# Spline stage with six result buffers, x added by a transfer, and one mask block in eight made on ScalarE

## The chip, the cores and the metric

The kernel runs on one core of one Trainium2 chip. The metric is the device time of one execution in microseconds (us). A core has TensorE (PE in the profile), VectorE (DVE), ScalarE (ACT), GpSimd (POOL) and SyncE (SP), each with its own instruction stream in program order. They share SBUF, wait for each other through semaphores, and data moves by DMA, which SP, ACT or POOL issue.

## The reference

The input x is 32 images of 64 channels and 56 x 56 pixels. Everything is float32.

```
out = relu(batchnorm(conv3x3(x, sign(w1))))          # statistics over all images
z   = relu(batchnorm(conv3x3(out, sign(w2))) + x)
u   = (clip(z * a + b, -1.5, 1.5) + 1) * 0.5 * 31     # a, b per channel
i, t = floor(u), u - floor(u)
y_nl = sum over 4 neighbours of table[channel, i + k] * cubic_k(t)
out = id_gain * z + y_nl + bias                       # per channel
```

The table of a channel is `alpha_table` (32 x 8) times that channel's row of `mix`. So the last layer is a cubic spline with 32 knots and a different table in each channel, applied to 6.4 million values.

## The kernel before

**Two convolutions, then the spline.** Images are taken in 16 pairs, 128 partitions = 2 images x 64 channels. Each convolution sums its taps in PSUM, and its result goes to a scratch array in DRAM (`y1_scratch`, `y2_scratch`). Both end in a short batch norm on VectorE. The second one's scale and bias are needed before any spline value can be made. At 427 us of 1252.8 the spline stage begins, and nearly all of the change is in it.

**Chunks.** The spline works on 32 chunks, each half of an image pair: 128 partitions x 1568 pixels. A chunk's value is a polynomial of third degree in the distance `offset` from one of 17 centres, with an extra cubic term for distances over 1 (`far`). The five coefficients (tables) of each pixel depend on which centre is nearest. They are found without a gather: 16 masks say whether the pixel lies past step s, and TensorE adds up mask times step height. The masks stand in four tiles ("quads") of 128 partitions x 4 blocks x 1568 pixels: a block holds 32 of the 128 (image, channel) rows, and the four groups of 32 partitions hold four different steps. For this the cell number of each pixel (`cell`) is first copied by 16 small DMAs into `cell4` (the spread).

**One table.** `product` (line 1177) multiplies a mask tile by diagonal weights in two parts (high and low half of the step). Tables NEAR and FAR use all four quads (128 matmuls each per chunk), SQ, LIN and VAL only the two edge quads (64 each). Two PSUM areas `tab` alternate, so table number n may begin only when VectorE has read table n-2 (`table_used`, line 1200). VectorE then computes with the sum, reading PSUM directly.

**VectorE's order for chunk c** (`body`, line 1149): VAL of chunk c-1 (1090), `finish` of c-1 (1121), `total` of c+2 (1016: y times scale plus x), `near_cube` (1067), `fixed` and `linear` of c+2 (1022, 1028), `far_cube` (1075), `far_part` (1083), both middle masks of c+1 (1045), SQ (1090), `near_part` (1098), `slope` (1105), `add_slope` (1113), `offsets` of c+2 (1037).

**ScalarE's order** (line 993): `far_distance` of c (961), `position` of c+2 (930), `far_square` (968), `cells` of c+2 (938), `distance_square` (975), `distance` of c+1 (954), two edge masks of c+1 as signs (982). A sign is -1 or 1 where a mask is 0 or 1. So the edge weights are half the step, and half of all such steps is added to the constant `first`.

**GpSimd** issues one accumulating DMA per chunk, which adds `far` to `lin` (919). `far_distance` of the next chunk overwrites `far` and waits for it to land. **SP** issues for each chunk the store of the chunk before, the loads of y (into `zbuf`) and x (into one of four `lin` buffers), then the 16 spread DMAs.

Of the kernel before, what the change touches and what calls it, by code (L numbers as in the profile page):

```python
# [49 lines left out]
QUAD_ORDER = MIDDLE_QUADS + EDGE_QUADS  # L50
QUADS_OF = (QUAD_ORDER, QUAD_ORDER, EDGE_QUADS, EDGE_QUADS, EDGE_QUADS)
GROUP = 32
BUFS = 4
# [32 lines left out]
def convolutions(nc, sem, keep, wts, par_dram, mix_t, alpha_t, x, y1, y2):  # L86
# [3 lines left out]
    with ExitStack() as ctx:  # L90
# [44 lines left out]
        stored = [sem(f"y_stored{b}") for b in range(2)]  # L135
# [36 lines left out]
        x_first = x[0]  # L172
# [52 lines left out]
        def _(sp):  # L225
# [60 lines left out]
            for b in range(2):  # L286
                sp.wait_ge(stored[b], 32 * half_rounds)

        @block.gpsimd
        def _(pool):  # L290
# [20 lines left out]
            for q in range(QUADS):  # L311
                for g in range(4):
                    above = SHIFT + 2 * (step_at(q, g) + 1)
                    link(pool.memset(thr[g * GROUP:(g + 1) * GROUP, q:q + 1],
                                     0.5 - above if q in EDGE_QUADS else above))
                    link(pool.memset(keep["above"][g * GROUP:(g + 1) * GROUP, q:q + 1], above))
# [25 lines left out]
            pool.wait_ge(steps_ready, 1)  # L342
            for t in range(TABLES):
# [13 lines left out]
        def _(act):  # L357
# [78 lines left out]
            act.activation(tmp[:, 5:6], row_scale[:, 0:1], ACT.Identity)  # L436
# [4 lines left out]
        def _(dve):  # L441
# [130 lines left out]
            def steps():  # L572
# [9 lines left out]
                link(dve.tensor_tensor(keep["first"][:, :], keep["plain"][:, :], halves[:, :], ALU.add), chain)  # L582
                for half in range(2):
# [193 lines left out]
def spline(nc, sem, keep, y2, x, out):  # L777

    with ExitStack() as ctx:
# [5 lines left out]
        cell4 = [sb(f"cell4{b}", [P, 4, CHUNK], BF16) for b in range(2)]  # L785
        edge_mask = [[sb(f"edge_mask{s}{q}", [P, 4, CHUNK], BF16) for q in range(len(EDGE_QUADS))] for s in range(2)]
        middle_mask = [sb(f"middle_mask{q}", [P, 4, CHUNK], BF16) for q in range(len(MIDDLE_QUADS))]
# [4 lines left out]
        dist_sq = sb("dist_sq", [P, CHUNK])  # L792
# [5 lines left out]
        stored = [sem(f"out_stored{b}") for b in range(BUFS)]  # L798
        far_added = sem("far_part_added")
        sum_ready = sem("sum_ready")  # L800
# [8 lines left out]
        dist_sq_ready = sem("dist_sq_ready")  # L809
# [16 lines left out]
        def summed(i, b, t):  # L826

            return tab[(b + t) % 2][:, :, 0:SUB]

        def mask_of(b, q):  # L830

            return edge_mask[b % 2][EDGE_QUADS.index(q)] if q in EDGE_QUADS else middle_mask[MIDDLE_QUADS.index(q)]

        def rounds(eng, body):

            def four(i, n):
                for b in range(BUFS):
                    body(i, b, n)

            last = CHUNKS // BUFS - 1  # L840
            four(0, 0)
            with eng.Fori(1, last) as i:
                four(i, None)
            four(last, last)

        def middle_masks(c):

            return (c + 1) * len(MIDDLE_QUADS) + len(EDGE_QUADS) if not isinstance(c, int) or c >= 0 else 0

        def edge_masks(c):  # L850

            return c * len(EDGE_QUADS) if not isinstance(c, int) or c >= 0 else 0

        def exists(n, b):
            return n is None or 0 <= BUFS * n + b < CHUNKS

        @block.sync
        def _(sp):
            def part(t, i, b):
                return in_front(sp, t[2 * i + b // 2][:, (b % 2) * CHUNK:(b % 2 + 1) * CHUNK])  # L860

            def load(i, b):

                ysrc = part(y2, i, b)
                xsrc = part(x, i, b)
                before, free = in_front(sp, BUFS * i + b - 1), in_front(sp, 16 * (i + b // BUFS))
                wait_past(sp, offset_ready, before)
                wait_past(sp, cell_ready, before)
                sp.dma_start(place[b % 2][:, :], ysrc).then_inc(y_loaded[b % 2], 16)
                wait_past(sp, stored[b % BUFS], free)  # L870
                sp.dma_start(lin[b % BUFS][:, :], xsrc).then_inc(x_loaded[b % BUFS], 16)

            def spread(i, b):

                c = BUFS * i + b
                made, used = in_front(sp, c + 1), in_front(sp, middle_masks(c - 2))
                used_edges = in_front(sp, edge_masks(c - 2))
                sp.wait_ge(cell_ready, made)
                wait_past(sp, mask_ready, used)
                wait_past(sp, sign_mask_ready, used_edges)  # L880
                first_two = isinstance(c, int) and c < 2
                for g in range(2 if first_two else 4):
                    for j in range(4):
                        sp.dma_start(cell4[b % 2][g * GROUP:(g + 1) * GROUP, j, :],
                                     cell[b % 2][j * GROUP:(j + 1) * GROUP, :]).then_inc(copied[b % 2], 16)

            def store(i, b):
                dst = part(out, i, b)
                made = in_front(sp, BUFS * i + b + 1)
                sp.wait_ge(whole, made)  # L890
                sp.dma_start(dst, lin[b % BUFS][:, :]).then_inc(stored[b % BUFS], 16)

            spread(0, 0)
            load(0, 2)
            spread(0, 1)

            def body(i, b, n):
                if exists(n, b - 1):
                    store(i, b - 1)
                if exists(n, b + 3):  # L900
                    load(i, b + 3)
                if exists(n, b + 2):
                    spread(i, b + 2)

            rounds(sp, body)
            dst, b = part(out, CHUNKS // BUFS - 1, BUFS - 1), BUFS - 1
            for half in range(2):
                own = slice(half * 2 * SUB, (half + 1) * 2 * SUB)
                sp.wait_ge(whole, CHUNKS + 2 * half + 1)
                sp.dma_start(dst[:, own], lin[b][:, own]).then_inc(stored[b], 16)  # L910
            for b in range(BUFS):
                sp.wait_ge(stored[b], 16 * (CHUNKS // BUFS + (b == BUFS - 1)))

        @block.gpsimd
        def _(pool):
            def add_far(c):

                pool.wait_ge(far_part_ready, 2 * c + 2)
                pool.dma_start(lin[c % BUFS][:, :], far[:, :], accum_op=ALU.add).then_inc(far_added, 16)  # L919

            for c in range(CHUNKS):
                add_far(c)
# [351 lines left out]
```

## Time and profile before

| | us |
|---|---|
| median of three runs | 1256.31 (1255.05 to 1257.22) |
| the profiled execution's own time | 1254.66 |
| its span in the trace | 1252.8 |
| VectorE busy | 1062.8 (85%) |
| TensorE matmuls busy | 1058.6 (85%) |
| ScalarE busy | 868.8 (69%) |
| GpSimd busy | 113.4 (9%) |
| TensorE's mean granted clock | 0.93 of full |

The page divides the span into 40 slices of 31.3 us. VectorE is at 5 to 8 tenths in the first third, which is the convolutions, and at 9 or more in nearly every slice after it. The granted clock of TensorE falls to 0.8 or 0.9 in the same slices. "Idle before, releaser" in a row is how long the engine stood still just before those instructions, and who ended that. Start times are us from the start of the span, and where instructions of one engine follow each other without idle time, the distance of two starts is a better price than the duration, as neighbours overlap slightly.

### The profile page before, as it was taken

The numbers are of one execution on the slowest core, as the hardware profiler recorded it, in microseconds if no ns is written. First come the engines' busy times: TensorE is split into PE (matmuls) and PEld (weight loads), VectorE is DVE, ScalarE is ACT, GpSimd is POOL, SyncE is SP. The second block draws the span as 40 slices with busy tenths as digits, with TensorE's granted clock in tenths as the row PEclk, the third lists the DMA queues.
The fourth block names the chain that finished last, engine by engine and source line by source line (L and its number), as shares of the span: only waits on it lengthen the run. The fifth ranks groups of instructions, "written<-read, shape, count | busy, mean of one in ns | idle before, by whom it ended". The sixth has DMA issues, their size and how long they took to land. (4 is left out here: it accounts for less than half of the span.)

```text
span 1252.8 us, 51454 instructions
## 1 busy us (share of the span) xinstructions
PE 1058.6 (85%) x23562; PEld 710.2 (57%) x23562; DVE 1062.8 (85%) x951; ACT 868.8 (69%) x424; POOL 113.4 (9%) x189
## 2 busy tenths in 40 slices
PE   6999996999999368887888788878887888788876
PEld 4688885788888234554545455444544545455444
DVE  5765656766666689999999999999999999999987
ACT  4454544777787267688868877887788778877881
POOL 6000000282000000000000000000000000000000
PEclk9999998999999778998989889898998989889898
DMA  7666766576777386677767766777677667776552
GB/s 227 259 257 256 276 255 225 217 277 252 271 264 300 136 235 181 183 216 194 185 189 213 196 181 193 208 192 184 189 214 192 184 197 206 194 182 197 157 114 78
DMA packets 58215, 260.85 MB, mean 208 GB/s; under 512 B 16336, under 2 KB 16336, under 8 KB 50000
## 3 DMA queue, kind: packets, MB, share of 16 engines
q1 hardware_dynamic: 52528, 230.88, 56.3%
q0 software_dynamic: 4608, 25.69, 11.0%
q8 instruction: 139, 2.28, 0.8%
q10 hardware_dynamic: 928, 1.90, 0.6%
q14 instruction: 12, 0.10, 0.0%
HBM read 104.29 MB, written 77.07 MB: 145 GB/s over the span
## 5 line engine op out<-in xcount | busy, mean ns | idle before, releaser
L1181 PE MATMUL tab<-edge_mask,diag 128*32 128x392 bf16 x10240 | 501.8, 358 | 132.6 <-DVE poly L1090 130.8
L1181 PEld LDWEIGHTS tab<-edge_mask,diag 128*32 128x32 f16 x10240 | 281.7, 104 | 339.0 <-DVE poly L1090 143.4
L982 ACT ACTIVATE edge_mask<-cell,thr 128x6272 bf16<-128x6272 bf16 x62 | 338.5, 5508 | 0.0
L711 PE MATMUL acc<-split,w 64*64 64x392 f16 x4608 | 195.9, 329 | 12.0 <-DVE w L463 10.8
L711 PE MATMUL acc<-band_split,w 64*64 64x392 f16 x4608 | 197.9, 330 | 9.4 <-ACT band_split L368 7.2
L410 ACT ACTIVATE yout<-acc 128x1568 f32<-128x1568 f32 x64 | 94.2, 1473 | 160.6 <-PE acc L711 139.4
L1181 PE MATMUL tab<-middle_mask,diag 128*32 128x392 bf16 x4096 | 183.4, 332 | 25.0 <-DVE middle_mask L1052 25.0
L711 PEld LDWEIGHTS acc<-band_split,w 64*64 64x64 f16 x4608 | 164.1, 107 | 42.9 <-issue 14.1
L711 PEld LDWEIGHTS acc<-split,w 64*64 64x64 f16 x4608 | 155.3, 107 | 51.9 <-issue 12.6
L520 DVE BATCH_NORM_STATS2 stats<-yout 128x392 f32 (+1 forms) x240 | 118.0, 555 | 60.2 <-ACT yout L410 59.4
L930 ACT ACTIVATE zbuf<-lin,cst 128x1568 f32<-128x1568 f32 x32 | 54.3, 1697 | 163.8 <-DVE lin L1016 157.9
L1181 PEld LDWEIGHTS tab<-middle_mask,diag 128*32 128x32 f16 x4096 | 107.7, 99 | 92.2 <-DVE middle_mask L1052 25.1
L919 POOL DMA_DIRECT2D lin<-far x32 | 50.0, 1564 | 897.5 <-DVE far L1083 897.5
L1090 DVE SCALAR_TENSOR_TENSOR poly<-tab,first,poly 128x1568 f32<-128x1568 f32 x61 | 112.6, 1845 | 0.1
L1045 DVE TENSOR_SCALAR middle_mask<-cell,thr 128x6272 bf16<-128x6272 bf16 x62 | 111.9, 1847 | 0.0
L486 DVE SCALAR_TENSOR_TENSOR band_split<-band_split,xin 128x1568 f16<-128x1568 f16 x30 | 52.5, 1793 | 35.0 <-ACT band_split L389 35.0
L1075 DVE SCALAR_TENSOR_TENSOR far<-tab,first,far 128x1568 f32<-128x1568 f32 x31 | 57.3, 1847 | 8.8 <-PE tab L1181 8.6
L497 DVE SCALAR_TENSOR_TENSOR split<-split,xin 128x3136 f16<-128x3136 f16 (+4 forms) x19 | 55.1, 2913 | 10.7 <-ACT split L400 10.5
L1083 DVE SCALAR_TENSOR_TENSOR far<-far,cst,far_sq 128x1568 f32<-128x1568 f32 x32 | 59.3, 1852 | 2.9
L1016 DVE SCALAR_TENSOR_TENSOR lin<-zbuf,cst,lin 128x1568 f32<-128x1568 f32 x32 | 59.0, 1846 | 3.1 <-PEq L90 3.1
L1121 DVE SCALAR_TENSOR_TENSOR lin<-poly,cst,lin 128x1568 f32<-128x1568 f32 x31 | 57.4, 1852 | 3.3
L1113 DVE SCALAR_TENSOR_TENSOR poly<-far_sq,poly 128x1568 f32<-128x1568 f32 x32 | 57.4, 1793 | 3.1
(126 smaller groups left out, 816.9 us busy)
## 6 DMA issues: line engine op xcount, KB each, us to landing
y_scratch<-yout SPq DMA_DIRECT2D x32, 1568.0 KB, 6.2
cell<-cell SPq DMA_DIRECT2D x496, 98.0 KB, 3.3
xin<-y_scratch SPq DMA_DIRECT2D x16, 1568.0 KB, 9.0
zbuf<-y_scratch SPq DMA_DIRECT2D x32, 784.0 KB, 5.9
lin<-in_x SPq DMA_DIRECT2D x32, 784.0 KB, 6.1
lin<-far POOLq DMA_DIRECT2D x32, 784.0 KB, 8.8
out<-lin SPq DMA_DIRECT2D x31, 784.0 KB, 4.1
xin<-in_x SPq DMA_DIRECT2D x15, 1568.0 KB, 9.3
```

The source lines that it names most:

```text
L410: act.activation(yout[b][:, :].rearrange("p (r k x) -> p k r x", r=2, k=TILES)[:, 2 * part:2 * part + 2], acc[:, 4 * part:4 * part + 4, 0: ...
L520: dve.bn_stats(stats[:, bass.ds(COUNTS * (g - base) + t, 1), :], yout[b][:, own]).then_inc(counted, 1)
L711: mm = pe.matmul(acc[h * C:(h + 1) * C, 2 * k + r, 0:TILE], weights[part][own, tap * C:(tap + 1) * C], image[own, first:first + ROWS, dx:d ...
L982: act.activation(mask_of(b, q)[:, :, :], cell4[b % 2][:, :, :], ACT.Sign, bias=thr[:, q:q + 1]).then_inc(sign_mask_ready, 1)
L1016: dve.scalar_tensor_tensor(out=lin[b % BUFS][:, :], in0=place[b % 2][:, :], scalar=cc(BN2_S), in1=lin[b % BUFS][:, :], op0=ALU.mult, op1=A ...
L1045: dve.tensor_scalar(mask_of(b, q)[:, :, :], cell4[b % 2][:, :, :], thr[:, q:q + 1], None, ALU.is_ge).then_inc(mask_ready, 1)
L1075: dve.scalar_tensor_tensor(out=quarters(far), in0=summed(i, b, T_FAR), scalar=base(i, b, T_FAR), in1=quarters(far), op0=ALU.add, op1=ALU.m ...
L1083: dve.scalar_tensor_tensor(out=far[:, :], in0=far[:, :], scalar=cc(AMP), in1=far_sq[:, :], op0=ALU.mult, op1=ALU.mult).then_inc(far_part_r ...
L1090: dve.scalar_tensor_tensor(out=quarters(poly[b % 2]), in0=summed(i, b, t), scalar=base(i, b, t), in1=quarters(poly[b % 2]), op0=ALU.add, o ...
L1113: dve.scalar_tensor_tensor(out=poly[b % 2][:, :], in0=far_sq[:, :], scalar=1 / POINT, in1=poly[b % 2][:, :], op0=ALU.mult, op1=ALU.add).th ...
L1121: dve.scalar_tensor_tensor(out=lin[b % BUFS][:, :], in0=poly[b % 2][:, :], scalar=cc(AMP), in1=lin[b % BUFS][:, :], op0=ALU.mult, op1=ALU. ...
L1181: mm = pe.matmul(tab[(b + t) % 2][j * GROUP:(j + 1) * GROUP, sub, 0:SUB], keep["diag"][part][:, j % 2, t, q, :], mask_of(b, q)[:, j, sub * ...
```

## The change

1. **Six result buffers.** `lin` has 6 buffers (`LIN`) instead of 4. For chunks 0 to 3 (`AHEAD`) y and x are loaded during the last convolution round, and VectorE still makes `total`. For every later chunk SP loads y straight into `lin`, ScalarE scales it in place (`scale`, new line 929), and GpSimd issues a second accumulating DMA that adds x from DRAM (`add_x`, new line 912). `position` waits for that instead of for `total`.
2. **One block of eight of the middle masks.** Block 3 of quad 3 is made on ScalarE as a sign (`shared`, new line 988). VectorE's mask of quad 3 shrinks from 6272 to 4704 elements per partition. TensorE uses the tile `shared_diag`, with half the step, for this block, and `first` gets the other half.
3. **Polynomial in another form.** `dist_sq` and ScalarE's `distance_square` are gone. VectorE adds SQ, multiplies by `offset`, adds LIN, multiplies by `offset`, adds VAL: as many instructions as before.
4. **Order.** On VectorE `finish` of c-1 comes after `linear`, and `fixed` before `near_cube`. On ScalarE the two edge masks are parted by `shared` and `distance`. On SP the store of c-1 comes after the spread of c+2 instead of before it. SP no longer waits, at the end of the convolutions, for their last stores to land. It waits for them in the spline stage behind two spreads.
5. **The rest.** The loops of the spline stage are written out. ScalarE's first activation is a square root instead of an identity. GpSimd prepares `shared_thr` and `shared_diag`, and VectorE does two small operations more in `steps`. The eight spread DMAs of chunk 1 that ScalarE issued are SP's.

```diff
@@ sync, last round of the second convolution
-                    sp.wait_ge(stored[0], 16 * (half_rounds + 1))
-                    for half in range(2):
-                        px = slice(half * CHUNK, (half + 1) * CHUNK)
-                        sp.dma_start(keep["zbuf"][half][:, :], y2[0][:, px]).then_inc(keep["y_loaded"][half], 16)
-                        sp.dma_start(keep["lin"][half][:, :], x_first[:, px]).then_inc(keep["x_loaded"][half], 16)
+                    for c in range(AHEAD):
+                        px = slice(c % 2 * CHUNK, (c % 2 + 1) * CHUNK)
+                        sp.wait_ge(stored[c // 2], 16 * (half_rounds + 1))
+                        y_to, x_to = keep["opening"](c)
+                        sp.dma_start(y_to[:, :], y2[c // 2][:, px]).then_inc(keep["y_loaded"][c], 16)
+                        sp.dma_start(x_to[:, :], x[c // 2][:, px]).then_inc(keep["x_loaded"][c], 16)
...
-            for b in range(2):
-                sp.wait_ge(stored[b], 32 * half_rounds)
@@ scalar, start
-            act.activation(tmp[:, 5:6], row_scale[:, 0:1], ACT.Identity)
+            act.activation(tmp[:, 5:6], row_scale[:, 0:1], ACT.Sqrt)
@@ spline, sync
+            def load(c):
+
+                if c < LIN:
+                    sp.wait_ge(sum_ready, AHEAD)
+                wait_past(sp, stored[c % LIN], 16 * (c // LIN))
+                sp.dma_start(lin_of(c)[:, :], image_half(y2, c)).then_inc(y_loaded[c % LIN], 16)
...
+            for c in range(CHUNKS):
+                if c + 4 < CHUNKS:
+                    load(c + 4)
+                if c + 2 < CHUNKS:
+                    spread(c + 2)
+                if c > 0:
+                    store(c - 1)
@@ spline, gpsimd
+            def add_x(c):
+
+                pool.wait_ge(scaled, c - AHEAD + 1)
+                pool.dma_start(lin_of(c)[:, :], image_half(x, c), accum_op=ALU.add).then_inc(x_added, 16)
...
             for c in range(CHUNKS):
+                if AHEAD <= c + 3 < CHUNKS:
+                    add_x(c + 3)
                 add_far(c)
@@ spline, scalar
+            def scale(c):
+
+                act.wait_ge(y_loaded[c % LIN], 16 * (c // LIN + 1))
+                act.activation(lin_of(c)[:, :], lin_of(c)[:, :], ACT.Identity, scale=cc(BN2_S)).then_inc(scaled, 1)
...
+            def shared(c):
+
+                act.wait_ge(copied[c % 2], 256 * (c // 2 + 1))
+                act.wait_ge(table_ready, used(c - 1, T_FAR))
+                act.activation(mask_of(c, SHARED_QUAD)[:, SHARED_BLOCK, :], cell4[c % 2][:, SHARED_BLOCK, :], ACT.Sign,
+                               bias=keep["shared_thr"][:, :]).then_inc(sign_mask_ready, 1)
@@ spline, vector
+            def times_offset(c, t, done):
+
+                dve.wait_ge(table_used, used(c, t))
+                dve.scalar_tensor_tensor(out=poly[c % 2][:, :], in0=offset[c % 2][:, :], scalar=1 / POINT,
+                                         in1=poly[c % 2][:, :], op0=ALU.mult, op1=ALU.mult).then_inc(done, 1)
@@ spline, tensor
+                        signed = c > 0 and (q, j) == (SHARED_QUAD, SHARED_BLOCK)
+                        weights = keep["shared_diag"][part][:, t, :] if signed else keep["diag"][part][:, j % 2, t, q, :]
```

VectorE, one chunk near the end of the spline stage, before (from `offsets` of one chunk to `far_part` and the masks, the numbers behind L are lines of the kernel before):

```order
L1037 TENSOR_SCALAR offset<-zbuf 128x1568
L1090 SCALAR_TENSOR_TENSOR poly<-tab,first,poly 128x1568
L1121 SCALAR_TENSOR_TENSOR lin<-poly,cst,lin 128x1568
L1016 SCALAR_TENSOR_TENSOR lin<-zbuf,cst,lin 128x1568
L1067 SCALAR_TENSOR_TENSOR poly<-tab,first,poly 128x1568
L1022 TENSOR_SCALAR zbuf<-zbuf,cst 128x1568
L1028 TENSOR_SCALAR lin<-lin,cst,par_sb 128x1568
L1075 SCALAR_TENSOR_TENSOR far<-tab,first,far 128x1568
L1083 SCALAR_TENSOR_TENSOR far<-far,cst,far_sq 128x1568
L1045 TENSOR_SCALAR middle_mask<-cell,thr 128x6272 x2
L1090 SCALAR_TENSOR_TENSOR poly<-tab,first,poly 128x1568
```

The same place on VectorE in the changed kernel, with its own line numbers (1084 adds a table, 1031 is `fixed`, 1063 `near_cube`, 1025 `linear`, 1097 `finish`, 1070 `far_cube`, 1077 `far_part`):

```order
L1038 TENSOR_SCALAR offset<-zbuf 128x1568
L1084 SCALAR_TENSOR_TENSOR poly<-tab,first,poly 128x1568
L1031 TENSOR_SCALAR zbuf<-zbuf,cst 128x1568
L1063 SCALAR_TENSOR_TENSOR poly<-tab,first,poly 128x1568
L1025 TENSOR_SCALAR lin<-lin,cst,par_sb 128x1568
L1097 SCALAR_TENSOR_TENSOR lin<-poly,cst,lin 128x1568
L1070 SCALAR_TENSOR_TENSOR far<-tab,first,far 128x1568
L1077 SCALAR_TENSOR_TENSOR far<-far,cst,far_sq 128x1568
L1046 TENSOR_SCALAR middle_mask<-cell,thr 128x6272
L1046 TENSOR_SCALAR middle_mask<-cell,thr 128x4704
L1084 SCALAR_TENSOR_TENSOR poly<-tab,first,poly 128x1568
```

`total` is gone, one mask is a quarter shorter, and `finish` has moved behind `linear`. From `far_cube` to the addition of SQ the sequence is otherwise the same.

ScalarE, one chunk before, then the same chunk in the changed kernel (969 `far_distance`, 940 `position`, 929 `scale`, 975 `far_square`, 948 `cells`, 981 edge masks, 988 `shared`, 963 `distance`):

```order
L961 ACTIVATE far<-poly,cst 128x1568
L930 ACTIVATE zbuf<-lin,cst 128x1568
L968 ACTIVATE far_sq<-far 128x1568
L938 ACTIVATE cell<-zbuf,cst 128x1568
L975 ACTIVATE dist_sq<-offset 128x1568
L954 ACTIVATE poly<-offset 128x1568
L982 ACTIVATE edge_mask<-cell,thr 128x6272 x2
```

```order
L969 ACTIVATE far<-poly,cst 128x1568
L940 ACTIVATE zbuf<-lin,cst 128x1568
L929 ACTIVATE lin<-lin,cst 128x1568
L975 ACTIVATE far_sq<-far 128x1568
L948 ACTIVATE cell<-zbuf,cst 128x1568
L981 ACTIVATE edge_mask<-cell,thr 128x6272
L988 ACTIVATE middle_mask<-cell,shared_thr 128x1568
L963 ACTIVATE poly<-offset 128x1568
L981 ACTIVATE edge_mask<-cell,thr 128x6272
```

ScalarE has one instruction more, and `position` now stands directly in front of `scale`.

## Rows read from the trace of the kernel before

**Rows 1.** The page, busy time of the span by engine.
```profile
PE 1058.6 (85%) x23562; PEld 710.2 (57%) x23562; DVE 1062.8 (85%) x951; ACT 868.8 (69%) x424; POOL 113.4 (9%) x189
```
**Rows 2.** Windows: length, busy of PE, PEld, DVE, ACT, POOL, clock, DMA share, GB/s.
```profile
600.00:1200.00 600.00, 497.42 (x10747) 291.30 (x10740) 587.26 (x361) 473.23 (x193) 38.09 (x24) 0.91 0.72 192
```
**Rows 3.** Timeline of VectorE, one chunk: start, duration, instruction, idle before.
```profile
803.68 1.85 DVE L1016 SCALAR_TENSOR_TENSOR lin<-zbuf,cst,lin 128x1568 f32<-128x1568 f32 x1
805.44 1.84 DVE L1067 SCALAR_TENSOR_TENSOR poly<-tab,first,poly 128x1568 f32<-128x1568 f32 x1
...
809.64 1.85 DVE L1075 SCALAR_TENSOR_TENSOR far<-tab,first,far 128x1568 f32<-128x1568 f32 x1 [0.25 <-PE tab L1181]
...
813.35 3.61 DVE L1045 TENSOR_SCALAR middle_mask<-cell,thr 128x6272 bf16<-128x6272 bf16 x2
816.88 1.85 DVE L1090 SCALAR_TENSOR_TENSOR poly<-tab,first,poly 128x1568 f32<-128x1568 f32 x1
...
828.93 1.85 DVE L1016 SCALAR_TENSOR_TENSOR lin<-zbuf,cst,lin 128x1568 f32<-128x1568 f32 x1
```
**Rows 4.** Timeline of TensorE, the same chunk.
```profile
818.78 4.52 PE L1181 MATMUL tab<-edge_mask,diag 128*32 128x392 bf16 x64 [3.89 <-DVE poly L1090]
823.12 2.83 PE L1181 MATMUL tab<-middle_mask,diag 128*32 128x392 bf16 x64
```
**Rows 5.** Timeline of VectorE, far_cube of chunk 0, then the stage's end.
```profile
459.44 1.85 DVE L1075 SCALAR_TENSOR_TENSOR far<-tab,plain,far 128x1568 f32<-128x1568 f32 x1 [1.04 <-PE tab L1181]
...
1209.51 1.85 DVE L1075 SCALAR_TENSOR_TENSOR far<-tab,first,far 128x1568 f32<-128x1568 f32 x1 [3.25 <-PE tab L1181]
...
1228.59 1.85 DVE L1067 SCALAR_TENSOR_TENSOR poly<-tab,first,poly 128x1568 f32<-128x1568 f32 x1 [0.69 <-PE tab L1181]
1233.89 1.85 DVE L1075 SCALAR_TENSOR_TENSOR far<-tab,first,far 128x1568 f32<-128x1568 f32 x1 [3.46 <-PE tab L1181]
```
**Rows 6.** Timeline of TensorE at the stage's end.
```profile
1218.64 4.52 PE L1181 MATMUL tab<-edge_mask,diag 128*32 128x392 bf16 x64 [3.95 <-DVE poly L1090]
```
**Rows 7.** Timeline of ScalarE, one chunk.
```profile
810.05 1.50 ACT L975 ACTIVATE dist_sq<-offset 128x1568 f32<-128x1568 int32 x1
...
812.86 10.93 ACT L982 ACTIVATE edge_mask<-cell,thr 128x6272 bf16<-128x6272 bf16 x2
823.68 1.59 ACT L961 ACTIVATE far<-poly,cst 128x1568 f32<-128x1568 f32 x1
830.81 1.70 ACT L930 ACTIVATE zbuf<-lin,cst 128x1568 f32<-128x1568 f32 x1 [5.53 <-DVE lin L1016]
```
**Rows 8.** Line 919 in 600 to 1200 us, issue to landing.
```profile
DMA to landing us min/median/max: 7.7/8.9/12.1
```
**Rows 9.** DMA queues in 600 to 1200 us: packets, bytes, share of 16 engines.
```profile
q1 hardware_dynamic: 28501, 94.74, 54.1%
q0 software_dynamic: 3456, 19.27, 17.3%
```
**Rows 10.** Timeline of GpSimd, its last two issues.
```profile
1213.59 1.59 POOL L919 DMA_DIRECT2D lin<-far  x1 [22.80 <-DVE far L1083]
1237.98 0.86 POOL L919 DMA_DIRECT2D lin<-far  x1 [22.80 <-DVE far L1083]
```
**Rows 11.** Timeline of SP's queue, one spread.
```profile
835.43 13.73 SPq L884 DMA_DIRECT2D cell<-cell  x16
```
**Rows 12.** Timelines of VectorE and TensorE, passage from convolution to spline.
```profile
424.20 0.22 DVE L624 SCALAR_TENSOR_TENSOR plain<-tmp,cst,plain 128x1 f32<-128x1 f32 x1
427.49 3.62 DVE L1016 SCALAR_TENSOR_TENSOR lin<-zbuf,cst,lin 128x1568 f32<-128x1568 f32 x2 [3.08 <-PEq L90]
...
446.43 4.92 PE L1181 MATMUL tab<-middle_mask,diag 128*32 128x392 bf16 x64 [24.98 <-DVE middle_mask L1052]
```
**Rows 13.** Timeline of VectorE, wait for the root in both batch norms.
```profile
212.89 0.16 DVE L650 RECIPROCAL tmp<-tmp 128x1 f32<-128x1 f32 x1 [0.98 <-ACT tmp L427]
...
422.22 0.16 DVE L650 RECIPROCAL tmp<-tmp 128x1 f32<-128x1 f32 x1 [0.25 <-ACT tmp L427]
```

More of the change, by code:

```diff
@@ L824, in quarters, with summed @@
             return t[:, :].rearrange("p (q x) -> p q x", q=4)
[L826 to L844, printed above, removed]
+        def summed(c, t):
+            return tab[(c + t) % 2][:, :, 0:SUB]
@@ L857, in _, with used, image_half, lin_of @@
+        def used(c, t):
+            return TABLES * c + t + 1
+        def image_half(t, c):
+            return t[c // 2][:, (c % 2) * CHUNK:(c % 2 + 1) * CHUNK]
+        def lin_of(c):
+            return lin[c % LIN]
         @block.sync
         def _(sp):
[L859 to L871, printed above, removed]
@@ L887, in store @@
[L887 to L903, printed above, removed]
@@ new lines, in store @@
+            def store(c):
+                sp.wait_ge(whole, c + 1)
+                sp.dma_start(image_half(out, c), lin_of(c)[:, :]).then_inc(stored[c % LIN], 16)
+            spread(0)
+            spread(1)
+            for b in range(2):
+                sp.wait_ge(keep["y_stored"][b], 16 * PAIRS)
+            for c in range(CHUNKS):
[5 more added lines that the diff above has]
+                    store(c - 1)
@@ new lines, in _ @@
+            for c in range(2):
+                position(c)
+                cells(c)
+                if c == 0:
+                    spread(c)
+            distance(0)
+            for c in range(CHUNKS):
+                far_distance(c)
+                if c + 2 < CHUNKS:
+                    position(c + 2)
+                if AHEAD <= c + 3 < CHUNKS:
+                    scale(c + 3)
+                far_square(c)
+                if c + 2 < CHUNKS:
+                    cells(c + 2)
+                if c + 1 < CHUNKS:
+                    edge(c + 1, EDGE_QUADS[0])
+                    shared(c + 1)
+                    distance(c + 1)
+                    edge(c + 1, EDGE_QUADS[1])
@@ L1070, in far_cube, with base, near_cube @@
-            def far_cube(i, b):
-                c = BUFS * i + b
+            def base(c, t):
+                return (keep["plain"] if c == 0 else first)[:, t:t + 1]
+            def near_cube(c):
+                dve.wait_ge(far_ready, c + 1)
+                dve.wait_ge(table_ready, used(c, T_NEAR))
+                dve.scalar_tensor_tensor(out=quarters(poly[c % 2]), in0=summed(c, T_NEAR), scalar=base(c, T_NEAR),
+                                         in1=quarters(poly[c % 2]), op0=ALU.add, op1=ALU.mult).then_inc(table_used, 1)
@@ L1172, in _ @@
-            rounds(dve, body)
+                    dve.wait_ge(table_used, used(c, T_VAL) + sub)
+                    dve.scalar_tensor_tensor(out=lin_of(c)[:, own], in0=poly[c % 2][:, own], scalar=cc(AMP),
+                                             in1=lin_of(c)[:, own], op0=ALU.mult, op1=ALU.add).then_inc(whole, 1)
+            total(0)
+            total(1)
+            for c in range(2):
+                fixed(c)
+                offsets(c)
+                linear(c)
+                total(c + 2)
@@ new lines, in _ @@
+            first_masks()
+            for c in range(CHUNKS):
+                if c > 0:
+                    add_table(c - 1, T_VAL, slope_ready, c)
+                if c + 2 < CHUNKS:
+                    fixed(c + 2)
+                near_cube(c)
+                if c + 2 < CHUNKS:
+                    linear(c + 2)
+                if c > 0:
+                    finish(c - 1)
+                far_cube(c)
+                far_part(c)
+                if c + 1 < CHUNKS:
+                    for q in MIDDLE_QUADS:
+                        middle(c + 1, q)
+                add_table(c, T_SQ, table_used, used(c, T_NEAR))
+                times_offset(c, T_SQ, near_ready)
+                add_table(c, T_LIN, near_ready, c + 1)
+                times_offset(c, T_LIN, slope_ready)
+                if c + 2 < CHUNKS:
+                    offsets(c + 2)
```

317 lines of the change are left out of this document (121 added, 196 removed).

## The prediction, on record before the run

> **What bounds the kernel now.** I read the page's busy line first [rows 1]: TensorE and VectorE are level at 85% of the span, so the average names no bound. The windows do: from 600 to 1200 us VectorE is busy 587 of 600 us, against 497 for TensorE and 473 for ScalarE [rows 2]. The timeline of one chunk shows VectorE without a gap, apart from 0.25 us before `far_cube` [rows 3]. One period, `total` to `total`, is 828.93 - 803.68 = 25.25 us there. Over the stage it is (1209.51 - 459.44) / 30 = 25.00 us [rows 5]. So VectorE's own work sets the period, but narrowly: that 0.25 us is already a wait for TensorE.
>
> TensorE has a loop of its own. VAL of chunk c may begin only when VectorE has read SQ of chunk c (two `tab` areas). Then TensorE does VAL, NEAR, FAR, and VectorE does `far_cube`, `far_part`, the middle masks, SQ, after which VAL of the next chunk may begin. In every period TensorE stands still for about 4 us before VAL [rows 4]. Its 64 matmuls of VAL then take 4.52 us, where the next 64 take 2.83: after that idle time part of them run at the lower clock (1.2 instead of 2.4 GHz; the mean granted clock of the stage is 0.91 [rows 2]).
>
> The price of this loop stands in the trace. At the end of the stage VectorE has no `total`, `fixed` and `linear` left to do, and so waits 3.25 and 3.46 us before `far_cube` [rows 5]. What remains is TensorE's loop alone: 1233.89 - 1209.51 = 24.38 us, only 0.62 us under the period of 25.00. VAL takes 4.52 us there too, after an idle time of 3.95 [rows 6].
>
> **The change part by part.**
>
> *VectorE's own work.* `total` goes: 805.44 - 803.68 = 1.76 us [rows 3]. The mask of quad 3 shrinks by a quarter. Two masks take 816.88 - 813.35 = 3.53 us, so one is 1.77 and its quarter 0.44 us [rows 3] (bounds: nothing, if time did not go by length, and 0.44; I take 0.44). The polynomial keeps its count. `near_part` and `add_slope` become products with the int32 `offset`; the kernel already multiplies by it in `slope`, at no visible extra. I take zero, with 0.1 us a chunk on either side. VectorE alone would come to 25.00 - 1.76 - 0.44 = 22.80 us.
>
> *TensorE's loop.* It contains `far_cube` to SQ, and of the change only the shorter mask lies inside: 24.38 - 0.44 = 23.94 us. The matmuls keep their number and shape, as the block with half weights only has another weight tile. This assumes that the clock still falls in the idle time, which shrinks from 3.95 to 3.51 us. If it never fell, VAL would be shorter by 4.52 - 2.83 = 1.69 us, the loop 22.25 us, and VectorE's 22.80 would bind. I take the falling clock, since 3.51 is near to 3.89 and 3.95, which have it. So the period is 23.94 us: the slower of two loops decides, and of VectorE's 2.20 us half comes back as waiting before `near_cube` and `far_cube`.
>
> *ScalarE.* From `dist_sq` through both edge masks to the end of `far_distance` it runs without a gap, and then it waits 5.53 us for `total` [rows 7]. So in a period of 25.25 it works 19.7 us. `distance_square` goes (1.50, or 1.4 by starts). `scale` comes (an activation of that size takes 1.50 to 1.70 [rows 7], I take 1.6). `shared` comes: a quarter of one edge mask is 10.93 / 8 = 1.37, a whole small activation 1.59; I take 1.5. Sum 19.7 - 1.4 + 1.6 + 1.5 = 21.4 us, under 23.94 by 2.5.
>
> *The loop through GpSimd's transfer.* `far_part` -> accumulating DMA -> `far_distance` -> `position` -> `fixed` -> `near_cube` -> `linear` -> `finish` -> `far_cube` -> `far_part`. `position` was held by `total` until now, so this loop is newly exposed. Its VectorE part is 809.64 - 805.44 = 4.20 (three of the four between), plus 1.76 for `finish`, plus 813.35 - 809.64 = 3.71 [rows 3], in sum 9.7. ScalarE adds 1.59 + 1.70 [rows 7], and 0.3 us pass before the issue. That is 13.3 us plus the landing. With the median landing of 8.9 [rows 8] it is 22.2 us, under 23.94; it binds from 10.6 on.
>
> *DMA.* x now comes by the software queue. There 24 adds took 17.3% of 600 us, 4.3 us of all 16 engines each. The hardware queue took 54.1% for 94.74 MB, so a plain x of 0.80 MB cost about 2.8 [rows 9]. All transfers of a chunk come to 0.72 x 25.0 = 18.0 us [rows 2], now 18.0 + 1.6 = 19.6 of 23.94, a share of 0.82. `add_x` has a whole period of slack before `position` needs it. SP's chain is the spread of 13.7 us [rows 11], the store behind it, the y load that waits for this store to land: even at the 8.9 us of the far add for that landing it is 22.6, also below 23.94.
>
> A rule of the Trainium skill speaks against a second software transfer. GpSimd's issue takes 1.59 us where VectorE makes masks beside it, and 0.86 us in the last chunk, which has none [rows 10]. SBUF — State Buffer, "Who interferes with whom" and its warning on software descriptors, says that GpSimd cannot write descriptors while VectorE runs in a two-port mode; the two issues agree with it. By the rule the add of x, which falls beside `fixed` and `linear`, would be issued about 1 us later, and with a period of slack the sum stays as it is.
>
> *The passage.* VectorE stands still for 3.08 us between batch norm and `total` [rows 12], which I put down to SP's wait for its last stores. It is gone, and I expect 2.4 us of it back (the other 0.7 for handing over between the stages is a guess). But VectorE now makes `total` of chunk 3 (1.76) before the first masks, on which TensorE waits. Gain 0.6 us (bounds 0 and 3.1). SP must now issue all 16 spread DMAs of chunk 1 itself, 13.7 us [rows 11], beside VectorE's masks of chunk 0 and TensorE's first two tables, which take 459.44 - 446.43 = 13 us [rows 5, 12], and more work follows before the copies are used.
>
> *The square root first.* VectorE waited 0.98 us for the first root and 0.25 us for the second [rows 13]; the difference, 0.7 us, is the loading of ScalarE's function table, which now happens at the start. ScalarE: Activation LUTs, "What ACT_TABLE_LOAD costs", has 2.66 us for a switch with its drain; by that the gain would be up to 2 us. The trace does not show so much, it shows 0.7. *`steps`* costs VectorE two small operations, 0.4 us, beside matmuls: I take 0.1.
>
> *Sum.* 30 periods x (25.00 - 23.94) = 31.8; the last period 0.4; passage 0.6; root 0.7; less 0.1: 33.4 us. The span is 1252.8 - 33.4 = 1219.4, and with the 1.86 us around it 1221.3. The profiled run was 1.65 us below the median of the three, inside their spread, so I predict 1221.
>
> **The rivals.**
>
> *A. TensorE's loop binds, 23.94 us: 1221.* For it: the period of 24.38 in the trace with VectorE waiting. Its own range is 1213 to 1230, which is 0.3 us a period either way, for how much of VAL falls into the lower clock (4.52 us is the case shown, all 64 at it would be 2 x 2.83 = 5.66, none 2.83) and for the quarter mask. Chance 0.60.
>
> *B. VectorE's own work stays the bound, 22.80 us: 30 x 2.20 = 66, 1187.* This needs the clock not to fall in a shorter idle time, at least mostly. Against it: both idle times shown, 3.89 and 3.95 us, are followed by it [rows 4, 6], and 3.51 is close. Halfway (one VAL in two at full clock) gives about 1204. Chance 0.12 for anything below 1213.
>
> *C. The far transfer lands later, but not by much.* Landing between 10.6 and 11.7 us gives periods of 24.0 to 25.0 and 1223 to 1252. For it: more traffic on the same queue, and single landings of 12.1. Against: the median must rise by 2 us, though the store has moved away from it. Chance 0.18, together with A's upper edge.
>
> *D. Slower than before: the same loop with landings over 11.7 us.* At 13 us the period is 26.3 and the time 1254.7 + 30 x 1.3 = 1294; at 12 us it is 1264. It decides from 11.7 us on, when `position`, `fixed` and `near_cube` start late one after the other and VectorE waits before `fixed`. Chance 0.08.
>
> *E. The change does not take the work off the path*, because ScalarE with 21.4 us of work and strict order falls behind: then TensorE would wait for `edge_mask`, at a period of 24.5 or more. Chance 0.02, about 1240.
>
> **How the numbers follow.** The likeliest is A, 1221. For 8 in 10 I reach into B and C: 1200 to 1241. What a measurement of this kernel can tell from no change is about 0.2%, 2.5 us. Faster are A, B and nearly all of C: 0.89. Within 0.2%: 0.02. Slower: D and the rest, 0.09.
>
> **What would show it.** VectorE waits for `tab` before `far_cube` in every chunk, 1 us or so with that before `near_cube`, and its busy share in the stage falls to about 0.95. VAL's 64 matmuls still take over 4 us, after 3.5 us of idle time. `far_cube` to `far_cube` is 23.9 us. ScalarE's long wait before `position` is gone, and a short one before `far_distance`, for the transfer, takes its place; `shared` is 1.4 to 1.6 us. The far transfer still lands in 9 to 10 us. I am wrong if VAL takes 2.8 us (B), if `fixed` waits for `position` (C, D), or if the passage grows.

## The result, and the profile after

| | before | changed |
|---|---|---|
| median | 1256.37 us (1255.05 to 1257.22, 4 runs) | 1221.07 us (1220.69 to 1225.48, 4 runs) |
| the profiled execution's own time | 1254.66 | 1220.8 |
| its span | 1252.8 | 1219.0 |

The ratio is 0.9728, with a 95% interval of 0.9704 to 0.9752: 2.7% faster. 1221 had been predicted.

The page of the changed kernel begins with the busy times of the engines, as in [rows 1]:

```profile
PE 1049.7 (86%) x23562; PEld 704.1 (58%) x23562; DVE 1003.0 (82%) x925; ACT 911.0 (75%) x450; POOL 143.6 (12%) x225
```

VectorE has lost 60 us of work, and the span is 34 us shorter. The stage from 600 to 1200 us shows where the others are, in the columns of [rows 2]:

```profile
600.00:1200.00 600.00, 513.24 (x11272) 301.25 (x11268) 557.11 (x347) 523.73 (x219) 60.03 (x47) 0.93 0.81 193
```

VectorE is busy for 557 us where it was for 587. The timeline of VectorE, one chunk (start, duration, instruction, idle time before it and who ended it), answers to [rows 3]. The first row is VAL, then come `fixed`, `near_cube`, `linear`, `finish`, `far_cube`, `far_part`, the masks, SQ, and after the gap in the rows the next `far_cube`:

```profile
809.15 1.84 DVE L1084 SCALAR_TENSOR_TENSOR poly<-tab,first,poly 128x1568 f32<-128x1568 f32 x1
810.91 1.08 DVE L1031 TENSOR_SCALAR zbuf<-zbuf,cst 128x1568 int32<-128x1568 f32 x1
812.59 1.85 DVE L1063 SCALAR_TENSOR_TENSOR poly<-tab,first,poly 128x1568 f32<-128x1568 f32 x1 [0.59 <-PE tab L1154]
814.35 1.09 DVE L1025 TENSOR_SCALAR lin<-lin,cst,par_sb 128x1568 f32<-128x1568 f32 x1
815.36 1.85 DVE L1097 SCALAR_TENSOR_TENSOR lin<-poly,cst,lin 128x1568 f32<-128x1568 f32 x1
817.89 1.85 DVE L1070 SCALAR_TENSOR_TENSOR far<-tab,first,far 128x1568 f32<-128x1568 f32 x1 [0.69 <-PE tab L1154]
819.78 1.85 DVE L1077 SCALAR_TENSOR_TENSOR far<-far,cst,far_sq 128x1568 f32<-128x1568 f32 x1
821.55 3.20 DVE L1046 TENSOR_SCALAR middle_mask<-cell,thr 128x6272 bf16<-128x6272 bf16 x2
824.66 1.84 DVE L1084 SCALAR_TENSOR_TENSOR poly<-tab,first,poly 128x1568 f32<-128x1568 f32 x1
...
841.78 1.85 DVE L1070 SCALAR_TENSOR_TENSOR far<-tab,first,far 128x1568 f32<-128x1568 f32 x1 [0.69 <-PE tab L1154]
```

VectorE now waits for TensorE twice in nearly every chunk, before `near_cube` and before `far_cube`, 1.28 us together in this one. The period is 841.78 - 817.89 = 23.89 us, and it is 23.89 or 23.90 from the seventh period on. The masks take 824.66 - 821.55 = 3.11 us instead of 3.53: the quarter mask is 0.42. TensorE in the same chunk (the answer to [rows 4]):

```profile
826.56 4.48 PE L1154 MATMUL tab<-edge_mask,diag 128*32 128x392 bf16 x64 [3.49 <-DVE poly L1084]
...
833.53 2.82 PE L1154 MATMUL tab<-edge_mask,diag 128*32 128x392 bf16 x64
```

It stands still for 3.49 us instead of 3.89, and VAL still takes 4.48 us, where the same number of matmuls takes 2.82 a little later. TensorE's granted clock in half microseconds there (length, busy time and matmuls, clock, DMA share, GB/s):

```profile
826.00:826.50 0.50, 0.00 (x0) 1.00 0.99 207
826.50:827.00 0.50, 0.44 (x8) 0.54 1.16 251
827.00:827.50 0.50, 0.50 (x12) 0.50 1.15 238
...
829.50:830.00 0.50, 0.50 (x12) 0.55 0.86 264
830.00:830.50 0.50, 0.50 (x20) 1.00 0.98 389
```

After 3.5 us without a matmul the clock goes to 0.5 (1.2 GHz) just as VAL begins, and comes back when TensorE has been busy throughout. The next 64 matmuls, with the clock at 1.00 (2.4 GHz), take the 2.82 us. ScalarE (the answer to [rows 7]) no longer waits 5.5 us for `total`. It waits for the far transfer instead:

```profile
830.91 1.60 ACT L969 ACTIVATE far<-poly,cst 128x1568 f32<-128x1568 f32 x1 [3.05 <-DMA lin<-far]
832.42 1.68 ACT L940 ACTIVATE zbuf<-lin,cst 128x1568 f32<-128x1568 f32 x1
834.01 1.59 ACT L929 ACTIVATE lin<-lin,cst 128x1568 f32<-128x1568 f32 x1
...
843.81 1.59 ACT L988 ACTIVATE middle_mask<-cell,shared_thr 128x1568 bf16<-128x1568 bf16 x1
```

The far transfer lands in 8.3 us, as quickly as before ([rows 8], 8.9), min/median/max in 600 to 1200 us:

```profile
DMA to landing us min/median/max: 6.6/8.3/10.2
```

**Where the 33.8 us of span came from**, by the start of `far_cube` in both traces. Up to chunk 0: 459.44 before, 460.14 now, 0.7 us lost. Chunk 0 to 30: 750.07 us before [rows 5], 1176.29 - 460.14 = 716.15 now, 33.9 gained. Chunk 30 to 31: 24.38 and 23.89, 0.5 gained. The end, from there to the span's end: 18.9 and 18.8, less than 0.1 gained.

### The profile page after: what moved, and what is told of

The parts are those of the page before. It is cut to its first block, busy times and chain, and to the rows that moved or that the text cites. A ratio compares the mean times of both kernels' runs of the same rounds, so it can differ in the third digit from the quotient of the medians.

```text
span 1219.0 us, 51044 instructions
## 1 busy us (share of the span) xinstructions
PE 1049.7 (86%) x23562; PEld 704.1 (58%) x23562; DVE 1003.0 (82%) x925; ACT 911.0 (75%) x450; POOL 143.6 (12%) x225
## 4 chain that ended last, share of the span: by engine, by line
PE 46%; DVE 15%; issue 3%; ACTq 0%; ACT 0%; DVEq 0%
PE tab L1154 46%; DVE middle_mask L1046 8%; DVE poly L1084 5%; ACTq L956 0%; DVE lin L1019 0%; DVE poly L1090 0%; DVE lin L1112 0%; DVE poly L1108 0%; DVE zbuf L1031 0%; DVE far L1070 0%; DVE middle_mask L1053 0%; ACT zbuf L940 0%; ACT cell L948 0%; DVE lin L1025 0%; DVE far L1077 0%
## 5 line engine op out<-in xcount | busy, mean ns | idle before, releaser
L1154 PE MATMUL tab<-edge_mask,diag 128*32 128x392 bf16 x10240 | 492.3, 354 | 107.9 <-DVE poly L1084 107.2
L1154 PEld LDWEIGHTS tab<-edge_mask,diag 128*32 128x32 f16 x10240 | 277.7, 103 | 311.6 <-DVE poly L1084 119.8
L1084 DVE SCALAR_TENSOR_TENSOR poly<-tab,first,poly 128x1568 f32<-128x1568 f32 x92 | 170.0, 1847 | 1.1
L1154 PEld LDWEIGHTS tab<-middle_mask,diag 128*32 128x32 f16 x3600 | 104.5, 98 | 90.9 <-DVE middle_mask L1053 24.9
L1090 DVE SCALAR_TENSOR_TENSOR poly<-offset,poly 128x1568 f32<-128x1568 int32 x64 | 114.7, 1792 | 2.2
L969 ACT ACTIVATE far<-poly,cst 128x1568 f32<-128x1568 f32 x32 | 51.4, 1606 | 78.4 <-DMA lin<-far 78.3
L1046 DVE TENSOR_SCALAR middle_mask<-cell,thr 128x6272 bf16<-128x6272 bf16 (+1 forms) x62 | 99.3, 1644 | 0.0
L1154 PE MATMUL tab<-middle_mask,shared_diag 128*32 128x392 bf16 x496 | 92.4, 329 | 0.0
L1063 DVE SCALAR_TENSOR_TENSOR poly<-tab,first,poly 128x1568 f32<-128x1568 f32 x31 | 57.4, 1851 | 18.6 <-PE tab L1154 18.6
L912 POOL DMA_DIRECT2D lin<-in_x x28 | 25.5, 910 | 341.5 <-ACT lin L929 341.5
```

The source lines that it names most:

```text
L1046: dve.tensor_scalar(mask_of(c, q)[:, own, :], cell4[c % 2][:, own, :], thr[:, q:q + 1], None, ALU.is_ge).then_inc(mask_ready, 1)
L1063: dve.scalar_tensor_tensor(out=quarters(poly[c % 2]), in0=summed(c, T_NEAR), scalar=base(c, T_NEAR), in1=quarters(poly[c % 2]), op0=ALU.ad ...
L1084: dve.scalar_tensor_tensor(out=quarters(poly[c % 2]), in0=summed(c, t), scalar=base(c, t), in1=quarters(poly[c % 2]), op0=ALU.add, op1=ALU ...
L1090: dve.scalar_tensor_tensor(out=poly[c % 2][:, :], in0=offset[c % 2][:, :], scalar=1 / POINT, in1=poly[c % 2][:, :], op0=ALU.mult, op1=ALU. ...
L1154: mm = pe.matmul(tab[(c + t) % 2][j * GROUP:(j + 1) * GROUP, sub, 0:SUB], weights, mask_of(c, q)[:, j, sub * SUB:(sub + 1) * SUB], start=( ...
```

## The experiments

Periods are the mean distance of `far_cube` from chunk 0 to chunk 31 in the profiled execution: 24.98 us before, 23.87 in the changed kernel. Times are medians. The kernel before, on the same chip each time, had 1254.7, 1255.9 and 1256.6 us in the three groups of runs.

### Is it TensorE's loop or VectorE's own work?

`extra784` gives VectorE more work outside TensorE's loop, `extra1568` twice as much:

```diff
@@ vector, in front of near_cube(c)
+                if c > 0:
+                    dve.wait_ge(table_used, used(c - 1, T_VAL))
+                    dve.scalar_tensor_tensor(out=spare[:, 0:784], in0=poly[(c - 1) % 2][:, 0:784], scalar=1.0,
+                                             in1=poly[(c - 1) % 2][:, 0:784], op0=ALU.mult, op1=ALU.add)
```

> The changed kernel with one more VectorE operation per chunk, 784 columns, 0.95 us, in front of near_cube and outside TensorE's loop; its result is not used. Theory: it fits in the 1.28 us that VectorE waits per chunk, period 23.9, time 1221 to 1223. Rival (VectorE's own work binds): 31 x 0.95 more, 1250.

> The changed kernel with an extra VectorE operation of 1568 columns (1.85 us) in front of near_cube, twice that of extra784. Theory: of it 1.28 us fit in the waits, 0.5 us show: period 24.4, time 1221 + 31 x 0.5 = 1236. If VectorE's own work bound already: 1221 + 31 x 1.8 = 1277.

Measured: 1220.6 us (period 23.87) and 1231.3 us (24.28). The first is free, as 0.9 us fit into the waits. The second makes VectorE the bound: most periods are 24.14 us, and VectorE's waits for TensorE in 480 to 1170 us are 3.4 us in sum, where the changed kernel has 34.0. One chunk of it, the extra operation and its neighbours:

```profile
914.70 1.09 DVE L1032 TENSOR_SCALAR zbuf<-zbuf,cst 128x1568 int32<-128x1568 f32 x1
915.70 1.79 DVE L1131 SCALAR_TENSOR_TENSOR spare<-poly 128x1568 f32<-128x1568 f32 x1
917.40 1.85 DVE L1064 SCALAR_TENSOR_TENSOR poly<-tab,first,poly 128x1568 f32<-128x1568 f32 x1
```

By starts the operation costs 1.70 us. So VectorE's own work in the changed kernel is 24.14 - 1.70 = 22.4 us, where the prediction had 22.80. That the first costs nothing speaks for TensorE's loop, as the added work lies outside it; had VectorE's own work been the bound, the time would have been 1250 us.

### Is the quarter mask on the path?

```diff
@@ vector, middle (and without shared(c + 1) on ScalarE; TensorE uses the full-step weights)
-                own = slice(0, SHARED_BLOCK if q == SHARED_QUAD else 4)
+                own = slice(0, 4)
```

> The changed kernel with the shared block undone: VectorE makes all four blocks of both middle masks (0.42 us more, inside TensorE's loop from far_cube to SQ), ScalarE makes no sign for it (1.5 us less). Theory 1, TensorE's loop as a plain sum: the period goes from 23.89 to 24.31 us and the time from 1221 to 1234. Theory 2, the loop is held by the clock: the low stretch begins at the same distance, VAL starts 0.4 us later in it, so a part of the low stretch falls into idle time and gives the delay back; period 23.9, time 1221 to 1224. Rival, VectorE's own work is the bound: it grows by 0.42 too, 1234, but then VectorE has no waits before near_cube and far_cube.

Measured: 1234.03 us, period 24.32. The time is that of theory 1, a plain sum: the quarter mask is worth 13 us, and the six buffers with all the rest 21 to 22 of the 35 (1254.7 - 1234.0 on the same chip). But the single periods are not those of a plain sum. In groups of eight they go 24.33, 24.33, 24.32, 24.11, 24.00, 23.95, 23.92, and then 25.59. TensorE's VAL in three chunks of such a group:

```profile
713.13 4.50 PE L1153 MATMUL tab<-edge_mask,diag 128*32 128x392 bf16 x64 [3.83 <-DVE poly L1083]
...
809.52 4.10 PE L1153 MATMUL tab<-edge_mask,diag 128*32 128x392 bf16 x64 [3.90 <-DVE poly L1083]
833.44 5.42 PE L1153 MATMUL tab<-edge_mask,diag 128*32 128x392 bf16 x64 [3.88 <-DVE poly L1083]
```

The low clock begins earlier against VAL from chunk to chunk, from 0.9 us after VAL's start to 0.8 before it, so ever more of it falls into idle time (4.50, 4.10), as theory 2 has it. Then a low stretch lasts twice as long as the others, all of VAL runs at the low clock (5.42), and the gain is lost. Theory 2 holds for some chunks and is wrong for the kernel. Why the mean comes to the plain sum of theory 1 isn't shown.

### What is the lower clock worth?

`fill96` gives TensorE extra matmuls behind LIN, in bank columns that nobody reads, and `before_fill96` does so in the kernel before. `f32fill60` has 60 in float32.

```diff
@@ tensor, table(c, t)
+                if t == T_LIN:
+                    for n in range(96):
+                        mm = pe.matmul(tab[(c + t) % 2][(n % 4) * GROUP:(n % 4 + 1) * GROUP, n // 4 % 4, SUB:BANK],
+                                       keep["diag"][0][:, 0, t, 1, :], mask_of(c, 1)[:, n % 4, 0:BANK - SUB],
+                                       start=True, stop=True)
                 mm.then_inc(table_ready, 1)
```

> The changed kernel, and TensorE issues 96 extra matmuls of 120 columns behind LIN, into columns of the PSUM banks that nobody reads, so that it stands still for about 1 us instead of 3.5 before VAL. Theory (the loop binds with its 1.7 us of lower clock): the clock no longer falls, VAL takes 2.8 us, the loop is 22.2 us, and VectorE's own work of 22.6 to 22.8 us binds: 30 x 1.1 less, about 1187. Rival (VectorE's work or the far transfer sets the period and the clock only fills idle time): 1221, or a few us more for the extra matmuls. If the transfers bind at this period, ScalarE waits for the far add over 3 us and the time is about 1200.

> The kernel before with the same 96 extra matmuls. Theory: VectorE's own work of 24.9 to 25.0 us binds there, so the full clock gives only the small waits back: 1251 to 1256, same. Rival (the lower clock was the bound before as well): 30 x 1.7 less, about 1205.

> The changed kernel with 60 extra float32 matmuls of 120 columns behind LIN, in place of the 96 bf16 ones that filled only 1.7 of 3.5 us. Expected fill about 3 us (4 passes each, four groups side by side: 50 ns), idle time before VAL under 1 us. Theory (clock after idle time binds, then the far transfer): no low stretches, VAL 2.8 us, every period at the 23.3 us that fill96 reached where the clock did not fall: 1221 - 30 x 0.58 = 1204. If VectorE's own work is next instead, 22.7 us and 1186. Rival (the clock is not on the path): 1221 or more.

Measured: `fill96` 1224.8 us, `before_fill96` 1253.95 us (ratio 0.9993, interval 0.9981 to 1.0004), `f32fill60` 1237.7 us. The kernel before does not change, as its VectorE bounds it. On the changed kernel my expectation failed, and the traces say why, in three parts. (1) The 96 matmuls usually last only 1.4 us, and 2.2 us of idle time are left before VAL. The clock still falls in most chunks, but not in all, after the same idle time:

```profile
659.29 2.84 PE L1154 MATMUL tab<-edge_mask,diag 128*32 128x392 bf16 x64 [2.22 <-DVE poly L1084]
...
682.59 4.52 PE L1154 MATMUL tab<-edge_mask,diag 128*32 128x392 bf16 x64 [2.23 <-DVE poly L1084]
```

(2) Where it does not fall, the period is 23.30 or 23.31 us, in `fill96` and in `f32fill60` alike, and not VectorE's 22.4. Something else binds at 23.30. (3) TensorE now stands still at times for nothing that the profile shows, as here in `f32fill60`:

```profile
813.62 3.16 PE L1154 MATMUL tab<-edge_mask,diag 128*32 128x392 bf16 x41 [3.18 <-issue]
```

From 480 to 1170 us such waits of TensorE are 0.7 us in the changed kernel, 22.5 in `fill96` and 29.1 in `f32fill60`. TensorE has 13% and 16% more matmuls (26,634 and 27,402 instead of 23,562; the profile counts each one in float32 as two), and the instruction queue's packets go from 139 to 163 and 169. A wait for instructions is one possible cause, but the count alone doesn't decide it: `before_fill96` has the same 26,634 matmuls and 163 packets and 3.1 us of such waits. What TensorE waits for wasn't tested and stays open.

### The transfer loop

`swap` lets ScalarE do `position` and `scale` in front of `far_distance`, and `swap_fill` adds the 60 float32 matmuls.

```diff
@@ scalar
-                far_distance(c)
                 if c + 2 < CHUNKS:
                     position(c + 2)
                 if AHEAD <= c + 3 < CHUNKS:
                     scale(c + 3)
+                far_distance(c)
```

> The changed kernel with ScalarE doing position and scale of the later chunks before it waits for the far transfer, instead of after. Theory (TensorE's loop of 23.89 us binds, the transfer loop of 22 to 23.3 us is only close): no change, 1219 to 1222. Rival (the transfer loop binds in part): up to 15 us faster.

> Both: position and scale first, and the 60 float32 matmuls. Theory: with the clock full and the transfer loop shortened by 3.3 us, VectorE's own 22.6 to 22.8 us is what is left: 1221 - 30 x 1.1 to 1.2 = 1186 to 1190, VectorE without waits. If the 23.3 us of fill96 were something other than the transfer loop, it stays at 1204.

Measured: `swap` 1221.7 us, no change, as the transfer loop did not bind at 23.9. `swap_fill` 1225.4 us, far over the 1186 to 1190 expected, with the clock full from 480 to 1170 us (granted 1.00), and again no period under 23.30. Its mean period is 23.92, in large part because TensorE stands still for 14.6 us without a visible cause there too (the same TensorE program had 29.1 in `f32fill60`). The full clock brought the period of 23.30 in about half of the chunks, but no shorter time. And 23.30 is neither VectorE's own work nor the transfer. `swap_fill`'s TensorE shows what it is:

```profile
824.03 2.84 PE L1154 MATMUL tab<-edge_mask,diag 128*32 128x392 bf16 x64 [0.40 <-DVE poly L1084]
827.74 1.50 PE L1154 MATMUL tab<-middle_mask,diag 128*32 128x392 bf16 x29 [0.88 <-DVE poly L1084]
```

There is a second wait, 0.88 us behind VAL, in front of NEAR. NEAR uses the PSUM area of LIN and may begin only when VectorE has added LIN. This loop runs from NEAR and FAR to `far_cube`, 815.36 - 804.29 = 11.07 us, and from `far_cube` over the masks, SQ and the product to the end of LIN, 827.69 - 815.36 = 12.33 us, in sum 23.4 (starts in `swap_fill`'s timelines: NEAR 804.29, `far_cube` 815.36, the end of LIN's addition 825.84 + 1.85). In the chunks whose period is 23.30 the first part is 10.92, and the sum is the period to 0.05 us. At the low clock VAL ends after LIN has been added (in the changed kernel NEAR begins at 830.88, and LIN is added at 828.37 + 1.85 = 830.22), so this wait is hidden. The prediction had only the loop through VAL.

### Shortening both loops

If two loops contain the masks, one mask moved behind LIN shortens both, and no instruction is added. `mask3_late` does that, `mask3_swap` adds the swap, and `masks_swap` moves both masks.

```diff
@@ vector, chunk c
-                    for q in MIDDLE_QUADS:
+                    for q in MIDDLE_QUADS[:1]:
                         middle(c + 1, q)
                 add_table(c, T_SQ, table_used, used(c, T_NEAR))
                 times_offset(c, T_SQ, near_ready)
                 add_table(c, T_LIN, near_ready, c + 1)
+                if c + 1 < CHUNKS:
+                    for q in MIDDLE_QUADS[1:]:
+                        middle(c + 1, q)
                 times_offset(c, T_LIN, slope_ready)
```

> The changed kernel with one instruction moved: VectorE makes the mask of quad 3 behind the addition of LIN instead of in front of the addition of SQ. Theory, two loops through the two PSUM areas: VAL after SQ (23.89 with 1.7 us of lower clock) and NEAR after LIN (23.3, seen with the full clock in swap_fill). Both lose the 1.35 us of this mask: 22.5 and 22.0. VectorE's own 22.6 us or the far transfer (13.3 us plus a landing of 8 to 10) is then the bound: period 22.7 to 23.2, time 1186 to 1200, though the clock may still fall. Rival (only the clock matters, as in the prediction's loop of one wait): the idle time moves between VAL and NEAR, the loss stays, 1221.

> mask3_late and ScalarE's position and scale in front of its wait for the far transfer. Theory: the transfer loop is off the path, VectorE's own work binds: period 22.6 to 22.7, time 1184 to 1188, and VectorE hardly waits. If the transfer did not bind in mask3_late, the two are the same.

> As mask3_swap, but both middle masks behind LIN. NEAR then waits for the first of them, and nearly all of TensorE's idle time (3 to 4 us) lies in front of NEAR. Theory: the clock falls there and its 1.7 us lie in the NEAR loop (22.0 + 1.7): period 23.7, time 1216. If the clock does not fall: 22.7 and 1187.

Measured: `mask3_late` 1198.9 us (period 23.05), `mask3_swap` 1181.9 us (22.57), `masks_swap` 1211.7 us (23.57). They came out in the order that the theory gave. `mask3_late` lies within what was expected, the other two 2 to 4 us under it. In `mask3_late` periods of 22.54 us stand beside longer ones, in which VectorE waits for `position`, and ScalarE, which makes it, for the far transfer. ScalarE's row in its timeline (the idle time before it in brackets, with who ended it):

```profile
801.50 1.60 ACT L969 ACTIVATE far<-poly,cst 128x1568 f32<-128x1568 f32 x1 [4.20 <-DMA lin<-far]
```

VectorE's row in the same chunk, which waits for what ScalarE does next:

```profile
804.73 1.10 DVE L1031 TENSOR_SCALAR zbuf<-zbuf,cst 128x1568 int32<-128x1568 f32 x1 [1.71 <-ACT zbuf L940]
```

So once TensorE's loops are shorter, the transfer loop does bind, and the swap that was worth nothing is now worth 17 us. `mask3_swap`'s engines from 600 to 1100 us, in the columns of [rows 2]:

```profile
600.00:1100.00 500.00, 436.76 (x9917) 267.79 (x9905) 491.68 (x311) 474.43 (x201) 62.77 (x45) 0.98 0.88 214
```

VectorE is busy for 492 of 500 us: it is the bound again, at 22.54 us, near the 22.4 that `extra1568` had given. The clock is at 0.98: it falls in about one chunk in three, and TensorE's idle time lies in pieces, up to 2.1 us before VAL and 0.9 before NEAR. That the parting keeps the clock up isn't shown: after a wait of 2.0 to 2.3 us before VAL it fell 8 times in 19 here, 9 in 17 in `mask3_late` and 12 in 17 in `fill96`. In `masks_swap` TensorE waits 2.73 us in front of NEAR in 29 chunks from 480 to 1170 us, its clock is at 0.94 and the usual period 23.72 (23.7 was expected):

```profile
824.08 2.36 PE L1157 MATMUL tab<-middle_mask,diag 128*32 128x392 bf16 x35 [2.73 <-DVE middle_mask L1046]
```

`mask3_swap` beats both kernels: the ratio to the kernel before is 0.9419 (0.9395 to 0.9444).

## Why the prediction was right, point by point

- **TensorE's loop binds (rival A): right.** Predicted period 23.94, measured 23.87. `extra784` shows it for itself: VectorE's added work is free.
- **The clock falls in the shorter idle time: right.** 3.49 us of idle time (3.51 predicted) and VAL at 4.48 us. VectorE's waits are 1.28 us a chunk (1 or so predicted), its busy share 0.93 (0.95).
- **VectorE's own work: 0.3 to 0.4 us too much.** 22.80 predicted, 22.4 to 22.5 measured. The difference was put to no use, as VectorE waits anyway. One part of it: `finish` began 1.98 us after VAL before, since it needs VAL's result, while now `fixed` begins 1.76 us after VAL.
- **The periods together: 33.9 us gained where 31.8 were predicted.** The first four periods are 23.57 to 23.85, under 23.89, and the later ones 0.05 under 23.94.
- **The passage and the square root: right, but a term is missing.** The root's wait went from 0.98 to 0.26 us as forecast: the table load in front of it, 1.28 us on ScalarE, is gone from there. The stop before `total` went from 3.08 to 1.01, 2.1 us instead of 2.4, and from the last batch norm's end to `far_cube` of chunk 0 there are 0.5 us less (460.14 - 425.39 against 459.44 - 424.20), where 0.6 was predicted. But this `far_cube` is 0.7 us later instead of 1.2 earlier. What is lost lies in the second convolution, for which the prediction had no term: from VectorE's reciprocal in the first batch norm to the one in the second it takes 423.40 - 212.46 = 210.9 us, against 422.22 - 212.89 = 209.3 before. It is 209.3 and 209.8 us in the two traces of the kernel before and 210.4 to 212.6 in the eleven of the changed kernel and its variants, so the change makes the second convolution 1 to 3 us longer. By what isn't shown. The start of `far_cube` itself lies anywhere from 458.9 to 462.6 us in those eleven, whose convolutions are the same, so one profile doesn't fix such a term to 1 us. That the sum came out to the microsecond is luck: two errors of 2 us with opposite signs.
- **DMA: the share right, the landing a little short.** A share of 0.81 (0.82 predicted); the far transfer lands in 8.3 us, where the sum had 8.9 and the signs 9 to 10. `shared` is 1.5 by starts, as predicted.
- **Rival B's price was wrong**, though B did not occur. It had 22.80 us with the full clock, but the loop through NEAR stops at 23.30. The clock, which the prediction held to be worth 1.1 us a chunk, is worth 0.6 in this order of instructions, and adding matmuls to keep it cost at least as much.
- **Rivals C and D**: the transfer loop was priced at 13.3 us and the landing. 0.25 us of that is the wait for TensorE in [rows 3], which 809.64 - 805.44 takes in. In the chunk of `mask3_late` shown, where this loop binds, it is 12.8 us (9.3 on VectorE from `fixed` to the end of `far_part`, 0.3 to the issue, 3.2 on ScalarE) and a landing of 11.3. In the changed kernel it bit in three chunks, where `fixed` waited 1.5 us in sum; in the 13 longer periods of `mask3_late` it waited 17.8.
- **Rival E**: ScalarE has 2.5 us a chunk left, as predicted (it waits 73.5 us for the far transfer in 29 chunks), and did not bind.

## What to carry to other kernels

When work is taken off the busiest engine, look for the loops that were a little shorter than its period, and write down what each contains: the same instruction is worth its full time inside such a loop and nothing outside. With buffers used in turn there is one loop for each buffer hand-over, so list all of them. Moving an instruction out of the loops (a mask that is needed only later) was worth 39 us here together with the swap, more than the change itself, at no added work.

## What the runs showed that was not expected

- The clock's loss does not add up chunk by chunk. With 0.42 us more in the loop the periods ran 24.33 down to 23.92 and then jumped to 25.59, with a mean of 24.32.
- Idle time of 2.0 to 2.3 us in front of VAL was followed by the low clock in 12 of 17 cases in `fill96` and in 8 of 19 in `mask3_swap`. So the length of this one stop does not decide it.
- 13% to 16% more TensorE instructions came with 15 to 29 us of waits without a visible cause in 690 us in variants of the changed kernel, but with 3 us in the kernel before.
- GpSimd's issue takes 1.59 us for adding far beside VectorE's masks, and 0.86 in the last chunk, which has none. For adding x it takes 0.87 us in 22 of 28 chunks and at most 1.25, so the 1 us that the prediction worked out for it by the rule did not come. SBUF — State Buffer of the Trainium skill, "Who interferes with whom", has the lock between VectorE's two-port mode and GpSimd; the far issues agree with it.
